# Attention units: three of eight through block transposes instead of four, and the raw output copied by ScalarE

## The reference, cut to what matters

```python
y = cond_ref(x, cond_8)                      # gated MLP of one expert for each batch
Q, K, V = y @ Wq.T + bq, y @ Wk.T + bk, y @ Wv.T + bv      # 16 heads of 8 channels
scores = einsum('bhqd,bhkd->bhqk', Q, K) / sqrt(8)
x_ = scores.transpose(0, 2, 1, 3).reshape(b * s, h, s)
x_ = conv_general_dilated(x_, conv_w, (1,), padding=[(1, 1)]) + conv_b  # 3 taps along the keys, mixes heads
weights = softmax(scores_from(x_), axis=-1)
out = einsum('bhqk,bhkd->bqhd', weights, V).reshape(b, s, e)
x = x + out @ Wo.T + bo
x = x + ffn_ref(cond2_ref(x, cond_8))        # LoRA layer, then 8 experts, top 1 with capacity 128
```

## Time and profile before

| | us |
|---|---|
| median of 3 runs | 273.62 (271.0 to 275.6) |
| profiled execution, its time | 270.89 |
| its span in the trace | 269.0 |
| TensorE busy (share of the span) | 232.8 (87%) |
| VectorE busy | 214.6 (80%) |
| ScalarE busy | 161.4 (60%) |
| GpSimd busy | 142.6 (53%) |

### The profile page before, as it was taken

The page is one execution under the profiler, slowest core; times in us unless marked ns, Lnnn a source line. Parts: engine busy times, 40 slices in busy tenths (PEclk is TensorE's granted clock), DMA queues, the critical chain, the costliest instruction groups (busy, mean ns, idle before and its releaser), DMA issues.

```text
span 269.0 us, 5140 instructions
## 1 busy us (share of the span) xinstructions
PE 232.8 (87%) x1595; PEld 172.9 (64%) x1595; DVE 214.6 (80%) x524; ACT 161.4 (60%) x292; POOL 142.6 (53%) x166
## 2 busy tenths in 40 slices
PE   8996979688887997888799869884998799999994
PEld 7455758465665765667567646572676576779982
DVE  2559998699988999899797999995799684686553
ACT  2743778677776678686776566675578480314321
POOL 1029888767788687688857547787383100000000
PEclk9998898999999999999999999998999999999999
DMA  7940007773657747555873707548727562500002
GB/s 222 378 180 0 0 12 238 224 158 159 154 213 197 195 175 156 202 130 186 261 157 122 182 15 238 153 142 251 156 117 184 199 130 68 246 0 0 2 2 78
DMA packets 13765, 39.58 MB, mean 147 GB/s; under 512 B 1458, under 2 KB 2994, under 8 KB 11570
## 3 DMA queue, kind: packets, MB, share of 16 engines
q1 hardware_dynamic: 13314, 38.69, 48.5%
q10 hardware_dynamic: 432, 0.65, 0.7%
HBM read 23.07 MB, written 16.25 MB: 146 GB/s over the span
## 4 chain that ended last, share of the span: by engine, by line
PE 41%; DVE 22%; DMA 21%; issue 8%; ACT 4%; SPq 2%; POOL 1%; DVEq 1%; ACTq 0%; POOLq 0%
DMA PT<-swap 11%; DVE Pb L538 9%; DMA swap<-w2s 8%; PE pvbank L827 7%; DVE w2s L669 4%; PE sc L809 4%; PE sc L811 3%; PE sc L810 3%; PE sc L1032 3%; PE tp L946 3%; PE tp L1042 3%; SPq L205 2%; DVE kc L482 2%; PE sc L992 1%; PE sc L771 1%
## 5 line engine op out<-in xcount | busy, mean ns | idle before, releaser
L345 ACT ACTIVATE Pb<-Pb,nbias 128x512 f32<-128x512 f32 x128 | 89.3, 719 | 55.6 <-DVE Pb L538 54.8
L538 DVE TENSOR_SCALAR_CACHE_REDUCE Pb<-sc,col 128x512 f32<-128x512 f32 x128 | 91.4, 737 | 8.1 <-PE sc L811 6.9
L809 PE MATMUL sc<-Kh,Ql 128*128 128x512 f32 x124 | 56.7, 457 | 8.6 <-issue 5.5
L242 POOL TENSOR_TENSOR Kl<-kc,Kh 128x512 fp32r<-128x512 f32 x29 | 37.4, 1291 | 37.6 <-ACT Kh L340 37.5
L811 PE MATMUL sc<-Kh,Qh 128*128 128x512 f32 x124 | 49.4, 398 | 0.0
L810 PE MATMUL sc<-Kl,Qh 128*128 128x512 f32 x124 | 49.1, 396 | 0.0
L827 PE MATMUL pvbank<-PT,Vst 128*32 128x256 f32 x480 | 30.6, 397 | 15.3 <-DMA PT<-swap 12.0
L254 POOL TENSOR_TENSOR td<-ta,tc_ 128x512 f32<-128x512 f32 x31 | 41.9, 1351 | 2.6
L669 DVE STREAM_TRANSPOSE w2s<-Pb 128x512 f32<-128x512 f32 x60 | 42.2, 704 | 0.0
L946 PE MATMUL tp<-cst,Pb 128*128 128x128 f32 x272 | 41.1, 275 | 0.6 <-ACT PT L389 0.5
L946 PEld LDWEIGHTS tp<-cst,Pb 128*128 128x128 f32 x272 | 33.8, 142 | 9.8 <-issue 1.4
(11 more groups left out here) (237 smaller groups left out, 269.1 us busy)
## 6 DMA issues: line engine op xcount, KB each, us to landing
swap<-w2s SPq DMA_DIRECT2D x15, 1024.0 KB, 3.9
PT<-swap SPq DMA_DIRECT2D x60, 256.0 KB, 4.8
w1s<-in_w SPq DMA_DIRECT2D x1, 2048.0 KB, 10.2
w2s<-in_w SPq DMA_DIRECT2D x1, 2048.0 KB, 8.0
cst<-in_consts SPq DMA_DIRECT2D x1, 648.0 KB, 5.7
xTs<-in_xT SPq DMA_DIRECT2D x2, 256.0 KB, 3.3
we<-in_wexp SPq DMA_DIRECT2D x2, 256.0 KB, 4.0
b2s<-in_b2row SPq DMA_DIRECT2D x1, 512.0 KB, 11.0
```

Source lines behind the costliest of these rows:

```text
L242: pool.tensor_tensor(Kl[:, n, :], kc[:, :], Kh[:, n, :].bitcast(f32), ALU.subtract)\
L345: act.activation(Pb[:, k, :], Pb[:, k, :], ACT.Exp, bias=nbias[:, k:k + 1], scale=-1.0)\
L538: dve.tensor_scalar(Pb[:, k, :], SC[k % 4][:, :], cb, None, ALU.subtract, ALU.min, accum_out=nbias[:, k:k + 1]).then_inc(s["mx"], 1)
L809: pe.matmul(SC[k][:, :], ql, Kh[:, h2, :], start=True, stop=False)
```

## The change

Of the four even units of a head pair, units 0, 2 and 4 still go through block transposes (`by_blocks`), unit 6 goes through TensorE and ScalarE like the odd ones; its eviction lands in a new area `PTC`. The five evicted units of a pair alternate between the two `TP` banks in their order 1, 3, 5, 6, 7 (`by_pe`). `TB`, `PTB` and the DRAM buffer shrink by a quarter, and SP starts a pair's transfer after the third block transpose. The write-after-read waits of `TB` are on the transfer to DRAM (`ts`) instead of the one back (`tm`). The output matmuls of each pair's second head take their 256 columns in two halves, since they lie in `PTB` and `PTC`. `raw_out` moves from VectorE, ahead of everything else at unit 8, to ScalarE, behind unit 8's `exp` and `Kh`. `by_token` moves on TensorE from unit 8 to 9, `normalise` on VectorE from unit 9 to 10. `TURN`, the unit at which the loops are cut, goes from 10 to 11.

```diff
+        half, cross_words = 8 * S, 4 * QT * 96
+        PTC = flat[:, half + 2 * cross_words:16 * S].rearrange("p (w k c) -> p w k c", w=2, k=QT)
...
+        def by_blocks(b, g, u):
+            return u % 8 in (0, 2, 4) and not last_pair(b, g, u)
+
+        def by_pe(b, g, u):
+            at = u % 8
+            return 10 * (NG * b + g) + 5 * (u // 8) + (at // 2 if at % 2 == 0 or at < 7 or last_pair(b, g, u) else 4)
...
             def cross(pair, w, gi):
-                sp.wait_ge(s["tb"], 4 * pair + 4)
+                sp.wait_ge(s["tb"], 3 * pair + 3)
...
+            def raw_out(b, g):
+                act.wait_ge(s["pv"], 2 * (NG * b + g) + 1)
+                act.wait_ge(s["otr"], NG * b + g)
+                act.activation(RAW[:, :], PV[:, :], ACT.Copy).then_inc(s["raw"], 1)
...
-                if u % 2 == 1:
+                if u % 2 == 1 or u % 8 == 6 and not last_pair(b, g, u):
+                    nth = by_pe(b, g, u)
+                    bank = TP[1 if last_pair(b, g, u) else by_pe(0, 0, u) % 2]
...
                 if u % QT == 0 and (not isinstance(g, int) or hd + 2 < B * H):
                     high_half(hd + 2, (u // QT) % 2)
+                if u == 8 and not (isinstance(g, int) and b + g == 0):
+                    raw_out(b, g)
...
-                    if u == 8:
-                        raw_out(b, g)
-                    elif u == 9:
+                    if u == 10:
                         normalise(b, g)
...
-                            x = PTA[:, 2 * w + i, k, :] if f else \
-                                PTB[:, w, :, k, 64 * i:64 * i + 64].rearrange("p i (t c) -> p t i c", t=2)
+                            if f:
+                                mm = pe.matmul(bank, v, PTA[:, 2 * w + i, k, :], **ends)
+                            elif i == 0:
+                                pe.matmul(bank, v, PTB[:, w, :, k, 0:64].rearrange("p i (t c) -> p t i c", t=2), **ends)
+                            else:
+                                t = k // 2
+                                for kk in (2 * k % QT, 2 * k % QT + 1):
+                                    x = PTC[:, w, kk, :] if t else PTB[:, w, :, kk, 64:96]
+                                    pe.matmul(bank[:, 128 * t:128 * t + 128], Vst[:, kk, 2 * w + i, :], x,
+                                              start=(kk == 0), stop=(kk == QT - 1))
...
-                if u == 8 and not (isinstance(g, int) and b + g == 0):
+                if u == 9 and not (isinstance(g, int) and b + g == 0):
                     by_token(b, g)
```

More of the change, by code:

```diff
@@ L30 @@
 AHEAD = 4
-TURN = 10
+TURN = 11
 AT_PE = {(0, 5): 12, (0, 10): 0, (0, 12): 2, (0, 14): 3, (1, 1): 6, (1, 3): 1, (1, 6): 7, (NG - 1, 10): 4,
@@ L143, in build @@
         flat = PT[:, :]
-        half = 8 * S
+        half, cross_words = 8 * S, 4 * QT * 96
         PTA = flat[:, 0:half].rearrange("p (g k c) -> p g k c", g=G, k=QT)
-        PTB = flat[:, half:2 * half].rearrange("p (w i k c) -> p w i k c", w=2, k=QT, i=4)
-        TB = w2s[:, :, :, :].rearrange("p e j c -> p (e j c)").rearrange("p (w i k c) -> p w i k c", w=2, k=QT, i=4)
-        PTX = TB[:, 1, :, :, :].rearrange("p i k c -> p (i k c)").rearrange("p (h k c) -> p h k c", h=2, k=QT)
+        PTB = flat[:, half:half + 2 * cross_words].rearrange("p (w i k c) -> p w i k c", w=2, k=QT, i=4)
+        PTC = flat[:, half + 2 * cross_words:16 * S].rearrange("p (w k c) -> p w k c", w=2, k=QT)
+        staging = w2s[:, :, :, :].rearrange("p e j c -> p (e j c)")
+        TB = staging[:, 0:2 * cross_words].rearrange("p (w i k c) -> p w i k c", w=2, k=QT, i=4)
+        PTX = staging[:, cross_words:cross_words + 2048].rearrange("p (h k c) -> p h k c", h=2, k=QT)
         Ub = [[flat[:, (4 * b + i) * 512:(4 * b + i + 1) * 512] for i in range(2)] for b in range(B)]
@@ L383, in unit @@
                     after(0, AT_ACT[g, u])
-                if u % 2 == 1:
+                if u % 2 == 1 or u % 8 == 6 and not last_pair(b, g, u):
+                    nth = by_pe(b, g, u)
+                    bank = TP[1 if last_pair(b, g, u) else by_pe(0, 0, u) % 2]
                     half_tile = u % QT // 2
[L387 to L390, removed]
+                    dst = PTA[:, u // QT % G, :, half_tile * 128:(half_tile + 1) * 128] if u % 2 else \
+                        PTC[:, u // 8, :, :]
+                    act.wait_ge(s["tp"], nth + 2)
+                    act.activation(dst, bank[:, :].rearrange("p (k q) -> p k q", k=QT), ACT.Copy)\
                         .then_inc(s["eva"], 1)
@@ L539, in maximum @@
                                   accum_out=nbias[:, k:k + 1]).then_inc(s["mx"], 1)
[L541 to L545, removed]
             def normalise(b, g):
@@ L649, in unit @@
                     over = isinstance(g, int) and G * g + m // QT >= H
[L650 to L653, removed]
+                    if not isinstance(g, int) or n >= 4:
+                        gone = (b, g, u - 4) if u >= 4 else (b, g - 1, u + U - 4)
+                        if by_blocks(*gone):
+                            dve.wait_ge(s["tb"], nth_blocks(*gone) + 1)
+                        elif last_pair(*gone) and u % 2 == 0:
+                            dve.wait_ge(s["tpx"], (u - 4 - U // 2) // 2 + 1)
+                        else:
+                            dve.wait_ge(s["tp"], by_pe(*gone) + 2)
                     maximum(n + AHEAD, m % RING, G * g + m // QT - (H if over else 0))
@@ L813, in outputs @@
             def outputs(pair, w, gi):
-                pe.wait_ge(s["eva"], 4 * pair + 5)
+                pe.wait_ge(s["eva"], 5 * pair + 6)
                 pe.wait_ge(s[f"tm{w}"], 64 * gi + 64)
@@ L824, in outputs @@
                             at = 32 * (2 * f + i)
-                            x = PTA[:, 2 * w + i, k, :] if f else \
-                                PTB[:, w, :, k, 64 * i:64 * i + 64].rearrange("p i (t c) -> p t i c", t=2)
-                            mm = pe.matmul(PV[at:at + VW, 256 * w:256 * w + 256], Vst[:, k, 2 * w + i, :], x,
-                                           start=(k == 0), stop=(k == QT - 1))
+                            bank, v = PV[at:at + VW, 256 * w:256 * w + 256], Vst[:, k, 2 * w + i, :]
+                            ends = dict(start=(k == 0), stop=(k == QT - 1))
+                            if f:
+                                mm = pe.matmul(bank, v, PTA[:, 2 * w + i, k, :], **ends)
+                            elif i == 0:
+                                pe.matmul(bank, v, PTB[:, w, :, k, 0:64].rearrange("p i (t c) -> p t i c", t=2), **ends)
+                            else:
+                                t = k // 2
[3 more added lines that the diff above has]
+                                              start=(kk == 0), stop=(kk == QT - 1))
                 mm.then_inc(s["pv"], 1)
@@ L931, in unit @@
                     scores(n + AHEAD, H * b + G * g + m // QT, b + 1 if over else b, m)
-                odd = U // 2 * gi + u // 2
-                if u % 2 or last_pair(b, g, u):
+                if not by_blocks(b, g, u):
                     pe.wait_ge(s["ex"], n + 2)
+                    nth = by_pe(b, g, u)
                     if last_pair(b, g, u):
@@ L939, in unit @@
                         else:
-                            pe.wait_ge(s["eva"], odd + u % 2)
+                            pe.wait_ge(s["eva"], nth + 1)
                     else:
-                        bank = TP[u // 2 % 2]
-                        if not isinstance(g, int) or odd > 0:
-                            pe.wait_ge(s["eva"], odd)
+                        bank = TP[by_pe(0, 0, u) % 2]
+                        if not isinstance(g, int) or nth > 0:
+                            pe.wait_ge(s["eva"], nth)
                     for k in range(QT):
@@ L947, in unit @@
                                           Pb[:, u % RING, k * 128:(k + 1) * 128], ident)
-                    mm.then_inc(s["tp" if u % 2 else "tpx"], 1)
+                    mm.then_inc(s["tpx" if last_pair(b, g, u) and u % 2 == 0 else "tp"], 1)
                 if u == U // 2 - 1 and not (isinstance(g, int) and b + g == 0):
@@ L1118 @@
     out = nc.dram_tensor("out", (T, C), mybir.dt.float32, kind="ExternalOutput").ap()
-    swap = nc.dram_tensor("swap", (128, 2, 4, 512), mybir.dt.float32, kind="Internal").ap()
+    swap = nc.dram_tensor("swap", (128, 2, 4, 384), mybir.dt.float32, kind="Internal").ap()
     build(nc, *args, out, swap)
```

10 lines of the change are left out of this document (6 added, 4 removed).

## The result

The changed kernel takes 278.85 us (278.72 to 279.12, 4 runs); the kernel before took 272.82 in the runs of that comparison. The ratio is 1.0245, with a 95% interval of 1.0183 to 1.0308: slower, though not by 2% for certain. Ratios and their intervals are taken from fast runs alone (slow ones are more than 1.5% above the fastest of their kernel), so a ratio isn't exactly the quotient of the medians beside it. The profiled execution took 278.89 with a span of 277.0, so 8.0 more than the 269.0 of before.

The account below looks back on a forecast made before the run. No engine's total decides: VectorE is fullest, but the `Kl` loop and the outputs' waits set the stretches. A +0.3, C +1.2 + 1.2, VectorE's full places -1.8 give +0.9 on 270.89: 271.8, said as 272; range 262 to 279.

Parts of the forecast that it names:

- the second rival: Units 7 to 10 and 15: late raw copy and split outputs cost in full, +3.6, +3, +1.5: 280 us; chance 0.17.
- B: Stretch from `kc` of unit 10 to unit 14: stays at 5.0 us, ScalarE's backlog worked off before index 16.
- A: Stretch from `kc` of unit 6 to 10, with w = 1 and raw outputs: 7.75 us each, six together +0.3.
- C: Stretch from `kc` of unit 14 to the next 2, over w = 0 outputs: +1.2 from starts, +1.2 from split outputs.
- start S: Outputs' start measured against the `kc` beside it: about -0.5 us in A and in C.
- the bank wait: Turn of unit 7 (15) needs unit 5's (13's) eviction, run behind `Kh`; late next after DMAs, start S about -0.5.
- D: Stretch from `kc` of unit 2 to 6, without outputs: closed loop through `Kl`, 5.24 us, unchanged with a longer `Kl` wait.
- The outputs' split: Outputs in 8 calls of 128 columns, not 4 of 256: +0.2 us each, +1.2 in six C; ends -0.05 and +0.5.
- VectorE's full places: Three places where VectorE has extra work and `kc` follows without idle: a removed transpose saves 0.6 each, -1.8 us.
- usual DMA waits are worth some 0.2 us of an A: Outputs in A: usual DMA waits cost some 0.2 us, the rare long one 3.6.
- VectorE's sum: Rival: a group shrinks by what leaves VectorE, 1.9 us: 258, or 264 if `Kl`'s loop passes half; chance 0.25.
- DMAs still binding: Rival: transfer not faster in its new place, start S in A +0.1 and more: 276 us; part of forecast's upper range.

Follow-up runs that it names:

- kc first: Changed kernel with `kc` of unit 10 made ahead of that unit's block transpose: 276.18 us, ratio 1.0072 to the kernel before.
- blocks only: Changed kernel with the raw copy back on VectorE at unit 8, turn at unit 8, normalisation at 9: 265.68 us, ratio 0.9693 to the kernel before.
- copy only: Kernel before with only the raw copy moved to ScalarE behind `exp` and `Kh`, its consumers one unit later: 285.22 us, ratio 1.0405.
- copy ahead: Changed kernel with ScalarE's raw copy moved ahead of unit 8's `exp` and `Kh`, consumers at units 9 and 10: 266.74 us, ratio 0.9735 to the kernel before.

## Why the prediction was wrong

I forecast 272 and no change; it is slower by 2.4%, close to the end of the second rival but not by all of its mechanism. The sum had +0.9 and the spans have +8.0; B holds 3.4 of the 7.1 between them, A 2.4, C 0.7, the rest 0.6.

*Right in mechanism and size.* The copy behind `exp` and `Kh`: `kc` comes 118.88 - 110.52 = 8.36 after the outputs' start, predicted 8.25; steady A 7.86 to 7.96, predicted 7.75. TensorE idles 1.58 for a predicted 1.7, VectorE 1.24 for 1.4. The start S by the bank wait, -0.4 for -0.5. D is closed, 5.25 as before. The outputs' split, which I took at 0.2, costs 0.04 (1.90 against 110.20 - 108.34 in the trace of before): two half-width calls in one column group cost nothing that shows, and the term of 1.2 for six C was too much. C's growth, 2.4 foreseen and 3.1 measured, has its causes right but for one: the first C fell by 1.1 for 1.2, the five that the bank wait lengthens grew by 3.3 for 2.4, and batch 1's first, not foreseen, by 1.0.

*The step that failed: "B ... stays at 5.0".* It grew to 5.5, by 3.4 in sum. I followed each wait in the shifted order, but priced `kc` by its length at its old time. Moved by a microsecond and a half it lands under `td`, and the loop of B begins with it: 1.38 - 0.89 = 0.49 in that group, 0.5 to 0.7 in the three steady ones and 0.2 and 0.4 in the last two, in each within 0.1 of the growth of `kc`'s own length. The run with `kc` first shows it. Batch 1's first group has 0.8; there the lower clock behind the copy wait (0.66 from 142 to 147 us) comes in, which I had priced at nothing: with `kc` first and a clock of 1.00 the same B is 6.06 instead of 6.98. And 0.3 lie in the first group, in blocks only and copy only as well, and have no cause that I can show.

*Also too small: A, six times 7.75.* The term +0.3 is +2.7. Steady groups exceed 7.75 by 0.1 to 0.2 only, but batch 1's three by 1.0, 0.7 and 0.3. The chain was worked out on a steady group; the first two of batch 1 carry batch 0's layers, and in the first of them TensorE waits 2.03 us for the copy instead of 1.58.

*The second: VectorE's full places, -1.8.* The rest of the stretches, D and everything outside of them, gave 1.2. But in batch 1's first group A, B and C grew by 0.9, 0.8 and 1.0. One of the two places there is real: its B is 5.53 in blocks only, 0.6 less than before. The late copy took that away again. Its C is 10.02 to 10.06 in every version with three of eight, evictions moved or not, and 9.04 to 9.06 in those with four. TensorE is busy 9.11 us of it instead of 7.99 and idles no longer than before, so the trace puts this 1.0 down to TensorE's extra work; no run separates it from ScalarE's. I had shown only that `kc` followed the transpose directly, not that the next wait was VectorE's.

*The third: "usual DMA waits are worth some 0.2 us of an A".* It rested on one A, that of 62.60. Without waits the A of 7.05 and 6.90 are 6.24 and 6.35, so 0.6 to 0.8 each, and C is 5.2, 10 us less in all. This didn't move the forecast of the sum much, as the bank wait takes C's share again, but it hid that the change's first half is a gain of 3% and the second a loss of 5%: 265.7 to 278.9.

*The rivals.* VectorE's sum: wrong; 15 transposes and the copy off it, and slower. Blocks only comes near its price by another cause, and the copy's 0.7 moved without a wait (copy ahead, 266.7) gives nothing over blocks only. The slower rival had the right place, units 7 to 10, but two of its terms, the split at 0.5 and a longer queue for the copy, didn't come, and A stayed under 8.5 but in batch 1's first group. Its third term did: against blocks only, A and B there grew by 3.9, 1.8 more than in the steady group shown, for the 1.5 named. DMAs still binding: wrong for the change, right for the copy alone.

What stays open: the kernel before ranged from 269.3 to 277.1 in 21 runs and the changed one only from 278.7 to 279.1 in four. Varying DMA waits fit, but the version without them still ranged from 258.5 to 260.9. The clock at the start has a share: kc first ranged from 274.6 to 277.1 in ten runs, in two clusters that go with the mean clock. Why the clock falls there in some executions and not in others, behind the same 2.17 us wait of TensorE, no run here shows.

## What to carry to other kernels

Moving an operation to an idler engine moves it in a queue: count what is ahead of it there from the event that feeds it, and who waits. Then lay the shifted operations beside the other engines' rows again, since one that shares a port with a neighbour has no fixed length. And where two edits come in one change, time them apart: here a gain of 3% lay under a loss of 5%.

## What the runs showed of the hardware

Two half-width matmuls in a row in one column group lengthen the outputs by only 0.04 us, with 40 matmul records in place of 32 and the same columns: 1.90 against 1.86 us. VectorE's `kc` (two inputs in SBUF) takes 0.71 to 0.75 us alone, 1.10 beside GpSimd's outer taps and up to 1.39 behind their sum; GpSimd's sum takes 1.29, and 1.74 when `kc` is first. Where a GpSimd operation runs as `kc` starts, `kc` ends 0.53 to 0.55 us behind it (three cases: the first outer tap in copy ahead at 106.55 and 112.96, the sum in the changed kernel at 118.88).

TensorE's granted clock fell behind waits of 1.95 to 3.64 us for DMAs, for ScalarE's copy and for VectorE alike, and outputs that stood in such a stretch took 2.7 to 3.5 us instead of 1.9. It did not fall each time: at the start of attention, behind 2.17 us of waiting, it fell in kc first and not in the changed kernel, where the code up to there is the same.
